# Routing, row scatters and weight splits placed inside the first attention, with split weights kept in DRAM

## The chip, the cores and the metric

One NeuronCore of one Trainium2 chip runs the whole kernel as one program. The metric is the device time of that core in microseconds (us); the time before is the median of three runs.

## The reference, cut to what matters

Two layers work on x of 8 batches x 256 x 512. The first layer, which the change is in, is a masked attention over 512 positions of width 256, and then a mixture of eight experts, of which every token takes two:

```python
x = x + _L0_ffn_ref(_L0_cond_ref(x, cond_2048, Wq, Wo), w_router, w_gate, w_up, w_down)

# the experts: 2048 tokens of width 512, E=8, F=352, K=2
probs = jax.nn.softmax(x @ w_router, axis=-1)
topk_w, topk_i = jax.lax.top_k(probs, K)
topk_w = topk_w / jnp.sum(topk_w, axis=-1, keepdims=True)
coef = jnp.einsum('tk,tke->te', topk_w, jax.nn.one_hot(topk_i, e, dtype=topk_w.dtype))
for ex in range(e):
    hid = jax.nn.silu(x @ w_gate[ex]) * (x @ w_up[ex])
    out = out + coef[:, ex:ex + 1] * (hid @ w_down[ex])
```

The second layer (another attention, then experts with low-rank additions) follows and is not changed.

## The kernel before, in words

The program is a row of blocks. In a block each of the five engines (TensorE, ScalarE, VectorE, GpSimd, SyncE) runs its own list of instructions in order, and they meet through semaphores; a block ends when all engines are through. Float32 values are multiplied as pairs of float16: a high half and the low rest, in three passes.

**`layer0_attention`** (from line 372) goes over 8 batches as a software pipeline. A batch has 32 slots. In a slot TensorE makes one bank of transposed scores (`pe_st`, line 226), ScalarE its exponential (`act_slot`, line 279), and every second slot TensorE multiplies with the values (`pe_pv`, line 239). Between the slots of batch b stand, by a list (`Core.plan`, line 91, used at line 403), steps of its neighbours. The natural scores of batch b+1 (`nat`: TensorE line 206, and VectorE takes each bank's row maxima, line 297) start at slot 10, 32 of them over the 22 slots left. The rest of batch b-1 has its slots too: reciprocal at 5, spread at 9, output projection at 11, row-major output (`rows`) at 13, router logits at 16. The query projections of b+2 are at 22 and 27. Natural and transposed scores have two banks each, and each engine keeps the order of the list, so an engine that stops holds up the others after two banks. The list is cut in two parts (at slot 18) because the loop body starts in the middle of a batch; steps of b-1 must stand ahead of the cut. SyncE's list for a batch is: load the inputs of b+2, put together its operand A (twelve DMAs, `assemble`, line 173), fetch the context of b (line 189). GpSimd puts together operand B. This kernel's attention writes row-major output for all 16 tiles of tokens to the tile `R` and the logits to `logits`.

**`layer0_routed`** (from line 729) is the next block. VectorE picks two experts for each token from all logits at once (`route_vector`, line 673, tiles of 128x128), TensorE ranks the tokens of each expert with triangular and full matrices of ones (lines 848 to 853), VectorE turns ranks into row numbers of the DRAM table `slots` and makes the table of tiles (lines 988 to 1013). GpSimd scatters the rows: 32 indirect DMAs (line 823), then 8 indirect pad writes (line 827), one behind each expert's rows. Beside this SyncE loads the weights of one expert after the other in float32 to a stage of one buffer per matrix (lines 775 to 783), ScalarE writes the high half (line 930), VectorE the low half (line 1018), and only then is the next expert's load issued. TensorE starts its first tile when all 24 low halves are made:

```python
pe.wait_ge(tabled, 1)
pe.wait_ge(consts_set, 15)
pe.wait_ge(w_lo, 3 * E)
turn_x(0)
```

SyncE issues the row loads (line 791) after its last weight load and when all scatters and pads have landed. Then come 39 tiles of 128 rows, each with two transposes, gate and up, down, and a scatter that adds to `x_rows` (line 838, GpSimd).

## Time and profile before

| what | value |
|---|---|
| median of 3 runs | 2172.78 us (2172.07 to 2174.30) |
| the profiled execution | 2166.6 us, span of its instructions 2164.5 us |
| TensorE busy | 1711.7 us (79%) |
| VectorE, ScalarE, GpSimd busy | 50%, 29%, 13% |
| DMA | 122.00 MB in 113344 packets |
| first attention | from about 11 to 525 us |
| joint: routing, splits, scatters | 525 to 623 us |
| routed tiles | 623 to 896 us |
| second layer | 896 us to the end |

The profile shows one execution. For each group of instructions it has busy time, the time of one, and what ended the idle time before. A timeline lists instructions in order of time, with merged runs of the same kind (x4 is four of them); "DMA to landing" is from a DMA's issue to its completion. PE is TensorE, ACT ScalarE, DVE VectorE, POOL GpSimd, SP SyncE; a trailing q is the engine's queue, L12 is line 12. The granted clock is in shares of TensorE's full 2.4 GHz.

### The profile page before, as it was taken

How to read it: one execution, taken by the hardware profiler on the slowest of the kernel's cores; microseconds unless marked ns; L12 is line 12 of the kernel's file. 1: busy time of each engine (PE TensorE's matmuls, PEld its weight loads, DVE VectorE, ACT ScalarE, POOL GpSimd, SP SyncE). 2: the span in 40 equal slices, each digit the busy share in tenths (PEclk: the TensorE clock that was granted, in tenths of full speed). 3: DMA queues.
4: the chain of work that ended last, by engine and by line, in shares of the span. 5: the costliest groups of instructions: out<-in, count | busy, mean ns of one | idle time of the engine just before them, and what ended most of it. 6: DMA issues, size and time to landing. Idle time of an engine off the chain costs nothing. (4 is left out here: it accounts for less than half of the span.)

```text
span 2164.5 us, 32950 instructions
## 1 busy us (share of the span) xinstructions
PE 1711.7 (79%) x10731; PEld 1023.2 (47%) x10731; DVE 1085.5 (50%) x2017; ACT 620.2 (29%) x1160; POOL 272.8 (13%) x343
## 2 busy tenths in 40 slices
PE   5888888885049999456777787795599999999998
PEld 1233333332026665232344443454477777777776
DVE  5455555542533333124455555553466665665665
ACT  0333333342332222131433333341321111111111
POOL 3111111100822222201111111000000000000000
PEclk7899999997569999756798998996699999999999
DMA  4122221101954444521111111014500000000000
GB/s 146 45 55 55 54 54 54 40 11 61 328 179 84 81 84 80 139 92 30 30 40 40 39 39 38 17 34 92 135 2 10 10 0 10 10 10 0 10 10 10
DMA packets 113344, 122.00 MB, mean 56 GB/s; under 512 B 40388, under 2 KB 79192, under 8 KB 113208
## 3 DMA queue, kind: packets, MB, share of 16 engines
q1 hardware_dynamic: 96872, 86.63, 14.1%
q0 software_dynamic: 15632, 34.30, 7.5%
q8 instruction: 43, 0.70, 0.1%
q14 instruction: 29, 0.24, 0.0%
q10 hardware_dynamic: 768, 0.13, 0.0%
HBM read 61.17 MB, written 29.96 MB: 42 GB/s over the span
## 5 line engine op out<-in xcount | busy, mean ns | idle before, releaser
L1768 ACT ACTIVATE d_SG<-d_bank 128x256 f32<-128x256 f32 x264 | 101.2, 383 | 381.0 <-PE d_bank L1705 301.9
L301 DVE TENSOR_REDUCE a_NM<-a_bn 128x1 f32<-128x512 f32 x256 | 163.4, 685 | 79.1 <-PE a_bn L215 75.6
L1803 DVE SCALAR_TENSOR_TENSOR d_HF<-d_bank,d_SG 128x256 f32<-128x256 f32 x264 | 112.1, 425 | 170.7 <-ACT d_SG L1768 152.3
L283 ACT ACTIVATE a_EX<-a_bt 128x512 f32<-128x512 f32 x256 | 143.9, 597 | 148.3 <-PE a_bt L234 147.9
L252 PE MATMUL a_bc<-a_EX,a_V 128*64 128x512 f32 x512 | 138.9, 621 | 0.0
L215 PE MATMUL a_bn<-a_B,a_A 97*128 97x512 f16 x256 | 98.3, 416 | 45.9 <-DVE a_NM L301 28.7
L1810 DVE TENSOR_TENSOR d_H_l<-d_HF,d_H_h 128x256 f16<-128x256 f32 x264 | 112.4, 426 | 9.3 <-DVE d_H_h L1808 0.4
L234 PE MATMUL a_bt<-a_A,a_B 98*128 98x512 f16 x256 | 90.7, 384 | 24.0 <-ACT a_EX L283 21.5
L301 DVE TENSOR_REDUCE c_NM<-c_bn 128x2 f32<-128x512 f32 x128 | 81.0, 681 | 42.2 <-PE c_bn L215 38.5
L862 PE MATMUL b_TX<-identh,R 128*128 128x128 f16 x312 | 24.3, 221 | 92.5 <-DVE b_wdl L1018 89.7
L1705 PE MATMUL d_bank<-XTl,d_wuh 128*128 x352 | 95.9, 273 | 0.0
L1705 PE MATMUL d_bank<-XTh,d_wuh 128*128 x352 | 95.9, 273 | 0.0
L1705 PE MATMUL d_bank<-XTh,d_wul 128*128 x352 | 95.9, 273 | 0.0
L1705 PE MATMUL d_bank<-XTh,d_wgh 128*128 x352 | 95.9, 273 | 0.0
L1705 PE MATMUL d_bank<-XTh,d_wgl 128*128 x352 | 95.9, 273 | 0.0
L1705 PE MATMUL d_bank<-XTl,d_wgh 128*128 x352 | 95.9, 273 | 0.0
L215 PEld LDWEIGHTS a_bn<-a_B,a_A 97*128 97x128 f16 x256 | 22.6, 98 | 154.4 <-DVE a_NM L301 114.0
L1230 PE MATMUL c_pp<-c_wqh,c_XNh 128*128 128x512 f16 x192 | 82.8, 431 | 12.5 <-DVE c_XNl L1340 7.8
L838 POOL DMA_INDIRECT x_rows<-R x39 | 60.5, 1550 | 224.7 <-DVE R L1028 220.8
L181 POOL DMA_DIRECT2D c_B<-c_H x64 | 35.2, 555 | 419.6 <-DVEq L1387 419.6
L1808 DVE CAST d_H_h<-d_HF 128x256 f16<-128x256 f32 x264 | 77.4, 293 | 16.1
L1668 POOL COPY d_EX<-d_kinds 128x1024 f32 x8 | 8.3, 1040 | 596.9 <-PE d_bank L1690 443.7
(346 smaller groups left out, 4044.7 us busy)
## 6 DMA issues: line engine op xcount, KB each, us to landing
R<-slot_rows SPq DMA_DIRECT2D x39, 264.0 KB
b_stage<-in_L_ffn_w_gate SPq DMA_DIRECT2D x8, 704.0 KB, 7.1
b_stage<-in_L_ffn_w_up SPq DMA_DIRECT2D x8, 704.0 KB, 7.0
a_xb<-in_x SPq DMA_DIRECT2D x8, 512.0 KB, 3.8
a_A<-a_H SPq DMA_DIRECT2D x64, 64.0 KB, 2.9
a_B<-a_H POOLq DMA_DIRECT2D x64, 64.0 KB, 2.6
a_CT<-a_CS SPq DMA_DIRECT2D x32, 128.0 KB
b_stage<-in_L_ffn_w_down SPq DMA_DIRECT2D x8, 512.0 KB
```

What stands on the lines that cost most here:

```text
L215: mm = nc.tensor.matmul(self.bn[s % 2][:, k * c.n:(k + 1) * c.n], A[0:c.k_nat, h, (t0 + k) * P:(t0 + k + 1) * P], B[0:c.k_nat, h, :], star ...
L234: mm = nc.tensor.matmul(self.bt[s % 2][:, k * c.n:(k + 1) * c.n], B[0:c.k_t, h, (t0 + k) * P:(t0 + k + 1) * P], A[0:c.k_t, h, :], start=Tr ...
L252: mm = nc.tensor.matmul(bank[64 * odd:64 * odd + 64, 0:c.n], self.V[n.par][:, t, h + odd, :], self.EX[(s + odd) % 4][:, k * c.n:(k + 1) * ...
L283: nc.scalar.activation(self.EX[s % 4][:, :], self.bt[s % 2][:, :], ACT.Exp).then_inc(self.exp_done, 1)
L301: self.nc.vector.tensor_reduce(self.NM[:, s * cols:(s + 1) * cols], self.bn[s % 2][:, :].rearrange("p (k n) -> p k n", k=cols), AX, ALU.ma ...
L838: Q.indirect_dma_start(out=g.xd[:, :], out_offset=bass.IndirectOffsetOnAxis(ap=XS[i % 4][:, E:E + 1].bitcast(I32), axis=0), in_=Y[i % 2][: ...
L1230: mm = nc.tensor.matmul(bank[:, :], xs[:, k, t * P:(t + 1) * P], ws[:, k, j * T0:(j + 1) * T0], start=(k == 0 and m == 0), stop=(k == KF - ...
L1705: mm = MM(b[:, w * CH:(w + 1) * CH], wt[s][:, k, f * P:(f + 1) * P], X[m][:, k, toks], start=(w == 0 and k == 0 and i == 0), stop=(k == KF ...
L1768: nc.scalar.activation(SG[k % 3][:, :], GU[(f + 3) % 4][:, 0:CH], ACT.Silu, scale=1.0 / WS).then_inc(silu, 1)
L1803: V.scalar_tensor_tensor(out=HF[:, :], in0=b[:, CH:2 * CH], scalar=1.0 / WS, in1=SG[k % 3][:, :], op0=ALU.mult, op1=ALU.mult).then_inc(mul ...
L1808: V.tensor_copy(H[0][:, :], HF[:, :]).then_inc(hi_step, 1)
L1810: V.tensor_tensor(H[1][:, :], HF[:, :], H[0][:, :], ALU.subtract).then_inc(hid, 1)
```

## The change

- Routing is done for one batch (two tiles of tokens) at a time, in the list of the attention. The steps of b-1 are now: `rows` at slot 12, `logit` at 14 (VectorE copies the logits and does 13 more steps to choose on 128x16 elements), `exp` at 18 (one exponential, two VectorE steps), `rank` at 21 (four matmuls, seven VectorE steps; a running count per expert is kept in `g.run`). The cut moves from slot 18 to 22.
- GpSimd makes the coefficients (five small operations) and scatters the four row tiles of b-1, waits until they have landed, and goes on to the operand of the next batch.
- Weights: in batch b the three matrices of expert b are split, by ScalarE and VectorE, at slots 1, 4 and 7. SyncE writes both halves to the DRAM table `expert_halves` and then loads the next expert's matrix; the first loads are issued after the assembly of batch 1.
- `layer0_routed` makes only the table of tiles. SyncE writes the eight pads as direct DMAs at a row number read from a register, when the table is there. ScalarE's queue loads the split weights with one DMA per expert from the start of the block, and TensorE waits for each expert's weights by a count that SyncE raises between its row loads.
- Tiles that shared the storage of `R` have their own storage now. The semaphores of the attention are cleared by GpSimd in the next block.

The diff, cut to its core:

```diff
-        plan = c.plan(18, {5: ("recip",), 9: ("spread",), 11: ("out",), 13: ("rows",), 16: ("logit",), 22: ("q0",), 27: ("q1",)},
+        plan = c.plan(22, {1: ("w0",), 4: ("w1",), 5: ("recip",), 7: ("w2",), 9: ("spread",), 11: ("out",), 12: ("rows",),
+                           14: ("logit",), 18: ("exp",), 21: ("rank",), 22: ("q0",), 27: ("q1",)},
                       ("shift", "values"))
...
+                def keep_weights(e, more=True):
+                    for i in range(3):
+                        sp.wait_ge(w_lo, 3 * e + i + 1)
+                        for h in range(2):
+                            sp.dma_start(g.halves[bass.ds(e, 1), :, h, W_AT[i]:W_AT[i] + W_SIZE[i]].rearrange("o p f -> (o p) f"),
+                                         part(h, i)).then_inc(w_kept[i], 16)
+                        if more:
+                            load_weights(e + 1, i)
...
                 a.assemble(sp, b1, a.A, a.a_in, (H, L, H))
+                sp.wait_ge(st_clear, 1)
+                for i in range(3):
+                    load_weights(0, i)
                 with sp.Fori(0, NB // 2 - 1) as i:
                     for q in range(2):
                         n = Batch(i, q + 2)
                         load(sp, n)
+                        keep_weights(2 * i + q)
                         a.assemble(sp, n, a.A, a.a_in, (H, L, H))
                         a.sp_context(sp, Batch(i, q))
...
+                    pool.wait_ge(rowed, n.idx + 1)
+                    pool.wait_ge(g.placed, n.idx + 1)
+                    pool.sem_inc(rows_begun, 1)
+                    for u in range(2):
+                        for k in range(2):
+                            Q.indirect_dma_start(out=g.slots[:, :],
+                                                 out_offset=bass.IndirectOffsetOnAxis(ap=r.place_i[:, 2 * n.par + k, u:u + 1], axis=0),
+                                                 in_=R[:, 2 * n.par + u, :], in_offset=None).then_inc(scattered, 16)
+                    pool.wait_ge(scattered, 64 * (n.idx + 1))
+                    pool.sem_inc(row_free, 1)
...
+                def split(n, i):
+                    act.wait_ge(st_in[i], (16, 16, 32)[i] * (n.idx + 1))
+                    act.wait_ge(w_kept[i], 32 * (n.idx + 1))
+                    nc.scalar.activation(part(0, i), stage[i][:, :], ACT.Copy, scale=WS).then_inc(w_hi, 1)
...
+                sp.wait_ge(tabled, 1)
                 for e in range(E):
...
+                    row = sp.value_load(r.pad_i[0:1, e:e + 1], min_val=0, max_val=E * REGION)
+                    sp.dma_start(g.slots[bass.ds(row, P), :], g.ZB[:, :]).then_inc(pads, 16)
+                sp.wait_ge(g.scattered, 64 * NB)
+                sp.wait_ge(g.pads, 32)
+                sp.wait_ge(pads, 16 * E)
+                ready = 0
                 for i in range(MT):
                     if i >= 4:
                         sp.wait_ge(added, 16 * (i - 3))
                     row = sp.value_load(r.tab[0:1, 0, i:i + 1], min_val=0, max_val=E * REGION)
                     sp.dma_start(XS[i % 4][:, :], g.slots[bass.ds(row, P), :]).then_inc(x_in[i % 4], 16)
+                    upto = (1, 1, 2, 3, 4, 6, 8)[min(i, 6)]
+                    for e in range(ready, upto):
+                        sp.wait_ge(w_in[e], 16)
+                        sp.sem_inc(w_ready, 1)
+                    ready = upto
...
                     e = pe.value_load(r.tab[0:1, 1, i:i + 1], min_val=0, max_val=E - 1)
+                    pe.wait_ge(w_ready, e + 1)
...
-                pe.wait_ge(w_lo, 3 * E)
                 turn_x(0)
...
+                for e in range(E):
+                    act.dma_start(W[:, e, :], g.halves[e].rearrange("p h f -> p (h f)")).then_inc(w_in[e], 16)
```

## Rows read from the trace of the kernel before

**Rows 1.** Table of stretches: from:to, length, busy (count) by engine, clock, DMA share, GB/s

```profile
175.00:230.00 55.00, 47.24 (x193) 16.23 (x193) 31.88 (x47) 22.39 (x40) 4.73 (x10) 1.00 0.14 37
...
533.00:623.00 90.00, 0.30 (x9) 0.24 (x6) 47.36 (x53) 32.33 (x24) 56.79 (x44) 0.50 0.87 311
...
560.00:580.00 20.00, 0.00 (x0) 0.00 (x0) 10.02 (x6) 7.66 (x7) 16.65 (x12) 0.50 1.02 374
...
623.00:896.00 273.00, 254.99 (x1833) 158.28 (x1831) 88.40 (x156) 74.70 (x118) 60.45 (x39) 0.99 0.41 73
```

**Rows 2.** Timeline of TensorE: start, us, line, tiles, [idle before <- releaser]

```profile
622.87 1.01 PE L862 MATMUL b_TX<-identh,R 128*128 128x128 f16 x8 [89.70 <-DVE b_wdl L1018]
```

**Rows 3.** Timeline of SyncE's DMA issues in the joint

```profile
525.85 0.43 SPq L775 DMA_DIRECT2D b_stage<-in_L_ffn_w_gate  x1
...
527.41 0.92 SPq L783 DMA_DIRECT2D b_stage<-in_L_ffn_w_down  x1
...
616.65 3.67 SPq L791 DMA_DIRECT2D R<-slot_rows  x4
```

**Rows 4.** Timeline of ScalarE in the joint

```profile
530.28 1.38 ACT L930 ACTIVATE b_wgh<-b_stage 128x1408 f16<-128x1408 f32 x1 [6.00 <-DMA b_stage<-in_L_ffn_w_gate]
...
535.89 1.48 ACT L930 ACTIVATE b_wdh<-b_stage 128x1536 f16<-128x1536 f32 x1 [1.80 <-DMA b_stage<-in_L_ffn_w_down]
```

**Rows 5.** Timeline of VectorE in the joint

```profile
538.01 0.18 DVE L979 TENSOR_TENSOR r_w<-r_w 128x16 f32<-128x16 f32 x1
...
538.22 0.29 DVE L980 TENSOR_TENSOR r_t<-r_oh,r_w 128x128 f32<-128x128 f32 x1
...
541.61 0.15 DVE L997 TENSOR_SCALAR r_cnt<-b_U 1x8 f32<-1x8 f32 x1
...
545.98 0.17 DVE L1013 TENSOR_SCALAR r_tab<-r_which 1x39 int32<-1x39 f32 x1
...
553.64 1.62 DVE L1018 SCALAR_TENSOR_TENSOR b_wgl<-b_stage,b_wgh 128x1408 f16<-128x1408 f32 x1 [2.75 <-ACT b_wgh L930]
```

**Rows 6.** GpSimd in the joint; then landings of line 817 and of line 838

```profile
528.04 0.63 POOL L817 DMA_DIRECT2D slot_rows<-b_ZB  x1 [0.30 <-POOL R L815]
...
543.16 1.10 POOL L823 DMA_INDIRECT slot_rows<-R,r_place_i  x1 [0.30 <-issue]
...
DMA to landing us min/median/max: 6.6/6.6/6.6
...
DMA to landing us min/median/max: 4.5/4.8/5.2
```

**Rows 7.** One attention batch: ScalarE's first exponentials, TensorE at slot 9, next batch

```profile
174.96 2.17 ACT L283 ACTIVATE a_EX<-a_bt 128x512 f32<-128x512 f32 x4 [6.13 <-PE a_bt L234]
...
182.61 1.08 PE L252 MATMUL a_bc<-a_EX,a_V 128*64 128x512 f32 x4
...
183.62 1.98 PE L264 MATMUL a_pp<-a_RV,a_SEL 8*128 8x512 f32 x4
...
233.13 2.16 ACT L283 ACTIVATE a_EX<-a_bt 128x512 f32<-128x512 f32 x4 [4.78 <-PE a_bt L234]
```

**Rows 8.** The same batch on VectorE: reciprocal and idle times before maxima and projection

```profile
179.39 3.34 DVE L322 RECIPROCAL a_RV<-a_RR 8x512 f32<-8x512 f32 x1 [5.45 <-DMA a_RR<-a_CS]
...
205.38 1.89 DVE L301 TENSOR_REDUCE a_NM<-a_bn 128x1 f32<-128x512 f32 x3 [1.18 <-PE a_bn L215]
...
208.11 1.29 DVE L301 TENSOR_REDUCE a_NM<-a_bn 128x1 f32<-128x512 f32 x2 [0.84 <-PE a_bn L215]
...
213.40 0.69 DVE L602 SCALAR_TENSOR_TENSOR a_QM<-a_pp,a_cb 128x512 f32<-128x512 f32 x1 [1.42 <-PE a_pp L488]
```

**Rows 9.** Batch 0: SyncE's last assembly DMA, and VectorE's first maximum after it

```profile
70.30 0.60 SPq L181 DMA_DIRECT2D a_A<-a_H  x1
...
75.99 1.29 DVE L301 TENSOR_REDUCE a_NM<-a_bn 128x1 f32<-128x512 f32 x2 [13.85 <-PE a_bn L215]
```

More of the change, by code:

```diff
@@ L106, in walk @@
 def walk(plan, table, b=None, b1=None, b2=None, last=None):
-    batch = {"first": b, "slot": b, "nat": b1, "shift": b1, "recip": last, "spread": last, "out": last, "rows": last, "logit": last}
+    batch = {"first": b, "slot": b, "nat": b1, "shift": b1, "recip": last, "spread": last, "out": last, "rows": last, "logit": last, "exp": last, "rank": last,
+             "w0": b, "w1": b, "w2": b}
     for name, *args in plan:
@@ L354, in batches @@
     walk(rest, steps, end, None, None)
-    walk([("recip",), ("spread",), ("out",), ("rows",), ("logit",)], steps, last=end)
+    walk([("recip",), ("spread",), ("out",), ("rows",), ("logit",), ("exp",), ("rank",)], steps, last=end)
 class Chain:
```

397 lines of the change are left out of this document (225 added, 172 removed).

## The prediction

> **What bounds the kernel now.** I read the stages first, then the engines across the joint between the first attention and the routed experts, then one batch of the attention. The table of stretches [rows 1] shows four things. In a batch of the attention TensorE is busy 47.2 of 55 us at full clock, so it is close to the bound. From 533 to 623 us it does nothing, while the DMA engines are at 0.87 of their time. At 560 to 580 they are full at 374 GB/s. From 623 to 896 TensorE is the bound again. So the joint is 90 us in which weights are loaded, split and rows scattered. Its end is set by the last low half of the weights: the first transpose of a row tile starts at 622.87, released by that split [rows 2]. All before it on the joint is the SP queue's loads [rows 3], two splits for each (ScalarE's and VectorE's [rows 4, 5]), and beside them 40 scatters on GpSimd [rows 6]. The change takes this work out of the joint. What it puts into the attention lands on engines that feed a TensorE with 7.8 us of slack in 55.
>
> **What the joint becomes.** Times are on the old axis, as if the attention had not grown. The last logits are out at about 525.2 (the routed block's first load issues at 525.85 [rows 3]). Then: 14 choosing steps (the logit copy among them) on 128x16 elements. A step and its wait take 0.21 us (538.01 to 538.22 [rows 5]), so 2.9, to 528.1; four small matmuls, 0.5, an estimate; seven ranking steps, 1.5, to 530.1; GpSimd starts at about 530.4. The exponential and GpSimd's coefficients run beside the ranking. Four scatters at 1.10 busy plus 0.30 [rows 6], 5.6, so the last is issued at 534.6; it lands 4.8 later if it is like the row additions [rows 6], 539.4, and GpSimd waits for that before the block ends. With 0.4 for the change of block the eight weight loads start at 539.8. The table of tiles is 17 steps: 15 run from 541.61 to 546.15 [rows 5], two more are 0.4, so it is there at 544.8. Then SP writes eight pads, each with a register load: the four row loads after 616.65 start 1.11 apart ((3.67 - 0.33)/3 [rows 3]; one issue is 0.33), so 8.9 us, to 553.7.
>
> **When the pads land** decides the sign. The first row load waits for them. Weights are 8 x 128 rows of 17,408 bytes, 17.8 MB, queued at once on ScalarE's queue from 539.8; the pads are 2.2 MB in rows of 2,112 bytes on SP's queue. The two ends: if both queues share by bytes, a pad lands in what the one plain pad write took beside loads, 6.6 us [rows 6], the last at 552.6 + 6.6 = 559.2, and with 3.5 for the first row load (0.7 at full rate, 2.5 fixed, see below, 0.3 to issue) the first transpose starts at 562.7, 60 us earlier than now. If a small write has to let a large transfer pass each time, the eight pads are through only with the eight weight loads: 20.0 MB at 374 GB/s [rows 1] is 53.5 us, 541 + 53.5 = 594.5, plus 3.5 gives 598, 25 us earlier than now. I take the second. The row that is nearest: the plain pad write of 264 KB was issued at 528.04, when 2.2 MB of loads had been issued from 525.85 to 528.3, and landed at 534.6 [rows 3, 6]. The last of those loads released ScalarE at 535.9 [rows 4]. All of it (2.75 MB with the second write) needs 7.4 us at 374 GB/s, to about 534.5. The first load, 704 KB alone, landed 4.4 after its issue [rows 3, 4], of which 1.9 is transfer at that rate, so 2.5 is fixed. An equal share by bytes would have had the pad write there in 1.4 + 2.5 = 3.9; it came out with the last of the loads. Here the rows in front are eight to twelve times longer still.
>
> The Trainium skill bears on this choice ("DMA: Bandwidth & Descriptors", Queues, rings and completion order): a DMA engine takes turns between its queues by whole packets, not by bytes, so long rows win against short ones; by that the first transpose is the one at 598. The same page's advice to prefer transfers of 1 MiB and more (Bandwidth) speaks for the change's one load per expert, and by it alone the one at 562.7 would hold. No row of this trace has rows of 17 KB beside short ones, so neither is shown here.
>
> **What the attention pays**, a batch at a time.
> (a) Weight halves on ScalarE at slots 1, 4 and 7: two of 1.38 and one of 1.48 [rows 4], 4.24 us. In slots 0 to 9 ScalarE's exponentials (ten of 0.54) fill 5.4 of the 7.65 us from 174.96 to the fifth pair of value matmuls at 182.61 [rows 7]. With the halves it is 9.65: these slots become ScalarE's, and TensorE is 2.1 us later. Bounds: 0.2 if the matmuls ran that much ahead (they can't: two banks of scores), 4.24 if all is exposed.
> (b) VectorE's low halves, 1.62 each [rows 5], lie in slots without maxima. But reciprocal and spread are there. The reciprocal began at 179.39 [rows 8] when its rows came. Now it stands behind the second low half, from 182.3 to 185.6; TensorE reaches the spread at 183.62 [rows 7] + 2.1 = 185.7, so it is covered, just. The third low half is behind it and makes the spread's product 0.4 late. That is the price of (b); without that cover it is up to 2.9.
> (c) The 14 choosing steps, 2.9 us where there was the one logit copy, now stand between two maxima. VectorE sat idle 1.18 before the maximum that follows the copy [rows 8]; the rest, 1.6, and 0.2 for waits and increments, goes to TensorE, which has two banks of natural scores and runs dry.
> (d) The two steps after the exponential, 0.45, fit the 0.84 that VectorE idles after an even slot [rows 8]: 0. The exponential itself is ready by then.
> (e) The seven ranking steps, 1.5, come where VectorE waits 1.42 for the query projection [rows 8]: 0.1, and 0.3 with TensorE's four matmuls.
> (f) GpSimd holds the four scatters from slot 21 to about 12 us later (5.6 plus 4.8 and the wait); the next batch's rows are assembled at slot 29, about 14 us after slot 21, so nobody waits: 0. If the scatters take 1.6 or more each the rows are late, but they have 8 us until slot 10.
> (g) SP: six writes, four loads and their waits end by slot 8; its next job is at slot 29: 0. The 4.4 MB a batch fit, since the DMA engines are at 0.14 [rows 1].
> Sum for each of batches 1 to 6: 2.1 + 0.4 + 1.8 + 0.1 + 0.3 = 4.7, 28.2 in all. Batch 7 has no maxima beside it: 2.6.
> (h) Batch 0 starts with nothing loaded: the loads of expert 0 stand on SP behind the assembly of batch 1, whose last DMA issues at 70.30 [rows 9]. So they issue at 71.0 to 73.3, and land as the first ones did, the first after 4.4, the last 8.5 after its issue [rows 3, 4]: 75.4 and 81.1. ScalarE has meanwhile stopped at slot 1. From 81.1 there are 1.48, two exponentials and the value matmuls, to about 85.0. Today the first maximum of the next batch is at 75.99, after its own wait of 13.85 [rows 9], from matmuls at 75.35. So 9.4, and 2 for the low clock after that pause, an estimate. With 0.4 for the added constant load at the start: 11.8.
> Attention: 28.2 + 2.6 + 11.8 = 42.6 us. Bounds: 20 (only batch 0 and 1 us a batch), 70 (splits, choosing and ranking all exposed, 9.1 on seven batches, less the cover of the waits).
>
> **The sum.** 42.6 lost, 24.9 won (622.9 - 598): 17.7 slower. The profiled execution has a span of 2164.5 and took 2166.6; the median of the runs is 2172.78, 6.2 above that, and I keep this distance. 2172.8 + 17.7 = 2190.5, rounded to 2190; the new profile's own time would be about 2184. The routed stage itself (273 us, [rows 1]) is unchanged: same matmuls, one more wait a tile, and weights that are all in by then.
>
> **Rivals.**
> Rival 1, on the other side: pads and row loads get through by share of bytes. Then the first transpose is 60 us earlier, at 562.7, and the place is the same pad wait on SP. Against it the pad row above; for it, that the trace never shows rows as long as these, so the slow end is carried over from one write. The weight loads would then run beside the first five or six tiles, whose additions already land only 4.8 after issue at 6.6 us a tile; I charge 4 us. 2172.8 + 42.6 - 56 = 2159.4, range 2148 to 2172. It decides from the point where the last pad lands before about 577, which is where the gain equals 42.6.
> Rival 2: the added steps hide better than I count, 20 us in the attention, with slow pads: 2172.8 + 20 - 25 = 2168. For it: each engine but TensorE is under 60% busy [rows 1]. Against: the waits are in sequence, with two banks.
> Rival 3: the scatters make the rows of the next batch late, or GpSimd and VectorE slow each other: 3 us more in six batches, 2190 + 18 = 2208. For it the uneven durations of scatters beside VectorE's long steps; against it the 8 us of slack in (f).
>
> **How the numbers follow.** Forecast 0.54 (2177 to 2204), rival 1 0.29, rival 2 0.09, rival 3 0.08. A measurement of this kernel tells about 0.2% (4.3 us) from no change. Faster: 0.26 of rival 1 and half of rival 2, 0.30. Same: 0.03 + 0.03 + 0.02 of the forecast, 0.08. Slower: 0.62. The range leaves out the lowest part of rival 1 and the upper half of rival 3: 2151 to 2207. The likeliest case's own range is 2177 to 2204.
>
> **What would show it.** In the changed profile: the last of SP's eight pads lands only when the weights' last load does (more than 40 us after the weights' start), and the first transpose follows it by 3 to 4 us; if it lands within 15 us of its issue, rival 1 holds. Batches 1 to 6 should last 63 us instead of 58.2 from one first exponential to the next (174.96 to 233.13 [rows 7]); in slots 0 to 9 the fifth pair of value matmuls comes 9.7 us after the first exponential; before the maximum that follows the choosing TensorE is idle near 2 us. Batch 0's slot 1 ends in a wait of some 14 us for the first gate weights. I am wrong in sign if the pads come early, and in size if a batch costs under 3 or over 7 us.

## The result, and the profile after

The changed kernel takes 2212.95 us (median of 4 runs, 2204.91 to 2214.55), the kernel before 2173.54 (2172.07 to 2174.89). The ratio is 1.0173, 95% interval 1.0153 to 1.0193: 39.4 us slower, where 17.7 was forecast. The sign was right; the time lies above the range (2151 to 2207). The two profiled executions have spans of 2212.6 and 2164.5, so 48.1 us are to be found in them; the profiled one is the slowest of its four, and the kernel's own runs differ by up to 10 us. Every ratio in the experiments is to runs of the kernel before that were made beside them (medians 2170.8 to 2173.3); "less" and "more" in us are against the changed kernel's 2212.95 and carry those few us of difference too.

First the joint, which answers to [rows 2 to 4]. Timeline rows of TensorE, SyncE and ScalarE; then the drains of GpSimd's queue at the end of the attention block (line of the block, duration in ns min/median/max, start in us), first before, then after; then issues and landings (KB each, median us):

```profile
668.04 1.01 PE L1018 MATMUL b_TX<-identh,b_XS 128*128 128x128 f16 x8 [72.61 <-DMA b_XS<-slot_rows]
620.48 8.22 SPq L977 DMA_DIRECT2D slot_rows<-ZB  x8
665.22 3.83 SPq L986 DMA_DIRECT2D b_XS<-slot_rows  x4
614.67 4.16 ACTq L1082 DMA_DIRECT2D b_W<-expert_halves  x8
...
L410 POOLq DRAIN  x1: 9716/9716/9716, 409.4 to 409.4; - x1
...
L431 POOLq DRAIN  x1: 9540/9540/9540, 604.9 to 604.9; - x1
...
b_W<-expert_halves ACTq DMA_DIRECT2D x8, 2176.0 KB, 26.7
slot_rows<-ZB SPq DMA_DIRECT2D x8, 264.0 KB, 26.6
...
slot_rows<-ZB SPq DMA_DIRECT2D x2, 264.0 KB, 36.2
```

What the DMA engines moved for the two queues from 625 to 660 us in the changed kernel (q10 has the weights, q1 the pads; packets, MB, share of the 16 engines):

```profile
q10 hardware_dynamic: 865, 13.39, 89.3%
q1 hardware_dynamic: 862, 1.62, 11.9%
```

The eight pads are issued from 620.5 to 628.7; the first lands after 10.2 us, the last two after 36.2, at 664.5, with the weights' last load. The two queues got the same number of packets (865 and 862), and the weights' packets carried eight times as many bytes (15.5 KB on the mean against 1.9): the pads did not wait for the queue of weights as a whole, they shared it packet by packet. The row loads go out at 665.2 and the first transpose is at 668.0. And GpSimd's queue drains for 9.54 us, from 604.9 to 614.5, while nothing else runs: every engine starts the routed block behind it. Before the change the same drain was at 409.4, under the attention.

Then the attention. Both fences below are tables of stretches as in [rows 1]. The first is six batches, from one shift-row store (ScalarE's DMA at line 187 before, 191 after, one a batch) to the sixth after it: before, and after.

```profile
111.74:458.17 346.43, 299.01 (x1224) 108.44 (x1223) 196.09 (x288) 134.42 (x240) 48.23 (x90) 1.00 0.18 47
...
120.44:521.03 400.59, 329.35 (x1248) 114.92 (x1247) 246.09 (x438) 157.70 (x264) 82.73 (x145) 0.93 0.39 123
```

Six batches last 54.2 us longer: TensorE idles 71.2 instead of 47.4 us (+23.8) and is busy 329.4 instead of 299.0 (+30.4), with only 24 more small matmuls. The last column but two tells why the busy time grew: the granted clock was 1.00, now it is 0.93 on the mean. Single batches after, the first of these six and the second, and one of the half-clock pieces in the second:

```profile
120.44:183.15 62.71, 51.33 (x210) 18.55 (x209) 41.59 (x74) 26.25 (x44) 14.30 (x26) 1.00 0.42 135
183.15:257.82 74.67, 60.73 (x211) 20.32 (x211) 41.72 (x74) 26.26 (x44) 14.10 (x26) 0.86 0.35 113
...
200.30:207.10 6.80, 6.80 (x15) 2.38 (x14) 3.15 (x5) 0.00 (x0) 0.00 (x0) 0.50 1.04 405
```

At full clock a batch lasts 62.7 (63 was forecast, 58.4 is its length before). In the second the clock falls to 1.2 GHz four times, for 3 to 7 us each, and one more thing is there: VectorE stands 3.4 us with nothing to wait for, and TensorE behind it (two rows each):

```profile
238.42 0.69 DVE L305 TENSOR_REDUCE a_NM<-a_bn 128x1 f32<-128x512 f32 x1 [3.42 <-issue]
374.08 0.69 DVE L305 TENSOR_REDUCE a_NM<-a_bn 128x1 f32<-128x512 f32 x1 [3.14 <-issue]
...
239.17 0.39 PE L219 MATMUL a_bn<-a_B,a_A 97*128 97x512 f16 x1 [2.43 <-DVE a_NM L305]
241.67 0.61 PE L219 MATMUL a_bn<-a_B,a_A 97*128 97x512 f16 x1 [1.89 <-DVE a_NM L305]
```

Both stalls begin, at 235.0 and 370.9, where the loop jumps back (the cut before slot 22), right behind the ranking steps. There is one at both jumps back of VectorE's loop and none where the loop is left.

The whole span: attention (to the last context load, 500.24 before, 567.05 after) +66.8; from there to the first transpose 101.0 where the forecast had 97.8 us, and 122.6 before, -21.6; routed stage, to the landing of the last row addition, +4.9; rest -1.9. Of the 4.9, the first tile at the lower clock takes 0.5 (8.5 us instead of 8.0 from one tile's first transpose to the next); most tiles last 6.69 us where they lasted 6.60, and some single ones over 7.5. The prediction had this stage unchanged, with one more wait a tile at no cost; no run tells whether that wait is the cause. Of the last -1.9, 1.8 is the drain of GpSimd's queue at the end of the routed block, which stands in the open in both kernels, before and then after:

```profile
L767 POOLq DRAIN  x1: 8401/8401/8401, 893.8 to 893.8; - x1
...
L971 POOLq DRAIN  x1: 6623/6623/6623, 943.8 to 943.8; - x1
```

### The profile page after: what moved, and what is told of

It is laid out like the page before. It is cut to its first block and busy times, and to the rows that moved or that the text cites. A ratio compares the mean times of both kernels' runs of the same rounds, so it can differ in the third digit from the quotient of the medians.

```text
span 2212.6 us, 33741 instructions
## 1 busy us (share of the span) xinstructions
PE 1743.5 (79%) x10731; PEld 1029.9 (47%) x10731; DVE 1104.0 (50%) x2167; ACT 617.8 (28%) x1167; POOL 260.9 (12%) x375
## 5 line engine op out<-in xcount | busy, mean ns | idle before, releaser
L219 PE MATMUL a_bn<-a_B,a_A 97*128 97x512 f16 x256 | 105.1, 438 | 58.6 <-DVE a_NM L305 47.4
L256 PE MATMUL a_bc<-a_EX,a_V 128*64 128x512 f32 x512 | 149.5, 665 | 0.0
L238 PE MATMUL a_bt<-a_A,a_B 98*128 98x512 f16 x256 | 100.0, 408 | 46.8 <-ACT a_EX L287 42.7
L1150 DVE SCALAR_TENSOR_TENSOR b_HF<-b_U,b_SG 128x352 f32<-128x352 f32 x39 | 20.4, 524 | 149.3 <-issue 88.0
L1004 POOL DMA_INDIRECT x_rows<-b_Y,b_XS x39 | 60.7, 1557 | 269.4 <-DVE b_Y L1141 260.0
L1033 PE MATMUL b_G<-b_W,b_XT 128*128 x468 | 78.2, 318 | 10.5 <-issue 10.5
```

What stands on the lines that cost most here:

```text
L219: mm = nc.tensor.matmul(self.bn[s % 2][:, k * c.n:(k + 1) * c.n], A[0:c.k_nat, h, (t0 + k) * P:(t0 + k + 1) * P], B[0:c.k_nat, h, :], star ...
L238: mm = nc.tensor.matmul(self.bt[s % 2][:, k * c.n:(k + 1) * c.n], B[0:c.k_t, h, (t0 + k) * P:(t0 + k + 1) * P], A[0:c.k_t, h, :], start=Tr ...
L256: mm = nc.tensor.matmul(bank[64 * odd:64 * odd + 64, 0:c.n], self.V[n.par][:, t, h + odd, :], self.EX[(s + odd) % 4][:, k * c.n:(k + 1) * ...
```

## Experiments on the joint

The theory at this point: the pads wait because the two queues take turns by rows, and GpSimd's drain stands in the open. The rivals: the pad stores are slow by themselves, or wait for the whole queue of weights.

**Pads and four rows ahead of seven weight loads.**

```diff
                 for e in range(E):
+                    if e == 1:
+                        for k in range(4):
+                            act.wait_ge(x_in[k], 16)
                     act.dma_start(W[:, e, :], ...).then_inc(w_in[e], 16)
...
-                    upto = (1, 1, 2, 3, 4, 6, 8)[min(i, 6)]
+                    upto = (0, 0, 0, 3, 4, 6, 8)[min(i, 6)]
```

> Edit: ScalarE issues expert 0's weights at once, the other seven only when the first four row loads have landed; all else as in the changed kernel (2212.95 us; pads issued at 620.5 to 628.7, the last landed at 664.5, first transpose at 668.0). Theory (turns): the pads are late because they share the DMA engines with 17.8 MB of long rows. Then each pad lands some 3 us after its issue, the first transpose is at about 635, and the seven loads run from 638 to 675 (15.6 MB at 430 GB/s). The fifth tile's row load falls under them and lands near 676 where the fifth tile began at 695 before: about 18 us less, 2195. Rival (the stores are slow by themselves, or SP's register loads hold them): the last pad still lands over 20 us after its issue, the first transpose stays near 660 to 668 and the weights come later on top: 2213 to 2230.

Measured: 2190.66 us, ratio 1.0079 (1.006 to 1.0098), 22 less than the changed kernel.

```profile
slot_rows<-ZB SPq DMA_DIRECT2D x8, 264.0 KB, 2.2
...
633.05 1.01 PE L1018 MATMUL b_TX<-identh,b_XS 128*128 128x128 f16 x8 [38.79 <-DMA b_XS<-slot_rows]
679.64 1.03 PE L1018 MATMUL b_TX<-identh,b_XS 128*128 128x128 f16 x8 [11.77 <-DMA b_XS<-slot_rows]
```

A pad now lands in 2.2 us. The stores are not slow by themselves: it was the weight loads. The price came where expected, a wait of 11.8 in the fifth tile.

**Short rows.** Weights in DRAM as 12 pieces of 1408 or 1536 bytes a partition, with gaps, loaded by four transfers an expert.

```diff
-        g.halves = dram("expert_halves", (E, P, 2, W_ALL), F16)
+        g.halves = dram("expert_halves", (E, P, 12, 800), F16)
...
+                    for h in range(2):
+                        at = h * W_ALL
+                        act.dma_start(W[:, e, at:at + 2 * GU].rearrange("p (c f) -> p c f", c=4),
+                                      g.halves[e, :, 6 * h:6 * h + 4, 0:GU // 2]).then_inc(w_in[e], 16)
+                        act.dma_start(W[:, e, at + 2 * GU:at + W_ALL].rearrange("p (c f) -> p c f", c=2),
+                                      g.halves[e, :, 6 * h + 4:6 * h + 6, 0:DN // 2]).then_inc(w_in[e], 16)
```

> Edit: the split weights lie in DRAM in rows of 1408 and 1536 bytes with gaps (17,408 bytes in one piece before) and are loaded by four transfers an expert; nothing else. Theory (a DMA engine takes turns between the two queues by rows, so the length of a row decides): the pads' rows of 2112 bytes now are the longer ones, each pad lands 3 to 5 us after its issue, first transpose at 636 instead of 668, the tiles then run beside the weight loads: 25 to 30 us less, 2185. Rival 1 (turns by whole transfers, or by bytes of a fixed chunk): the last pad lands some 10 to 20 us after issue, first transpose 645 to 655. Rival 2 (the later queue simply waits until the earlier one is empty): no change, last pad with the last weights, 668 to 672.

Measured: 2203.35 us, ratio 1.0156 (1.0117 to 1.0194), only 10 less.

```profile
slot_rows<-ZB SPq DMA_DIRECT2D x8, 264.0 KB, 5.8
...
635.03 1.01 PE L1018 MATMUL b_TX<-identh,b_XS 128*128 128x128 f16 x8 [46.41 <-DMA b_XS<-slot_rows]
...
656.27 1.64 ACTq L1086 DMA_DIRECT2D b_W<-expert_halves  x1
657.96 1.02 ACT L1094 ACTIVATE b_XT<-b_TX 128x1024 f16<-128x1024 f16 x1 [69.42 <-issue]
```

The theory of turns holds: with shorter rows beside them the pads land in 5.8 instead of 26.6 us (3 to 5 were expected), and the 865 packets beside 862 in the changed kernel say the same. The Trainium skill's rule of turns by whole packets ("DMA: Bandwidth & Descriptors", Queues, rings and completion order) agrees. That the first transpose came at 635.0 where 636 was expected is partly luck. In this run the block began 6.8 us earlier (first weight load issued at 607.9 instead of 614.7), so from there to the first transpose it took 27.2 us, where the expectation had 21.3 and the changed kernel 53.4. But the time didn't follow: 32 issues take ScalarE until 657.9 (before, eight took 4.2 us): the first nine take 0.4 to 1.7 us each, the tenth 5.8, and from there on they go out about as fast as the transfers themselves (12 MB in 37 us). The copy of the first tile stands behind them on the same engine. The gain went into a new wait; this I had not seen.

**GpSimd's last scatters behind the block's end.** The last batch's coefficients and four scatters move to the start of the routed block.

```diff
                 route(Batch(NB // 2 - 1, 0))
-                route(Batch(NB // 2 - 1, 1))
...
+                head = R[:, 2:4, :]
+                did(Q.tensor_copy(head[:, :, E:E + 1]..., last.token[:, :]))
+                did(Q.tensor_tensor(last.c[:, :, :], last.oh2[:, :, :], each(last.ex[:, :]), ALU.mult))
+                did(Q.tensor_tensor(last.c[:, :, :], last.c[:, :, :], last.oh1[:, :, :], ALU.add))
+                did(Q.tensor_tensor(head[:, :, 0:E], last.c[:, :, :], each(last.inv[:, :]), ALU.mult))
+                for u in range(2):
+                    for k in range(2):
+                        Q.indirect_dma_start(out=g.slots[:, :], ..., in_=R[:, 2 + u, :], in_offset=None).then_inc(g.scattered, 16)
```

> Edit: GpSimd's work for the last batch (coefficients, four scatters) stands at the start of the routed block instead of at the end of the attention block. In the changed kernel GpSimd's drain at the block's end takes 9.54 us (604.9 to 614.5) and everything waits for it. Theory (hidden drain): GpSimd ends the attention block under the last batch, its drain is covered, the routed block starts some 0.4 after the last placement (597.2) instead of at 614.7, the weight loads end 17 us earlier, the scatters hide behind the pads: 2213 - 17 = 2196. Rival (the drain is a cost of the block's end itself, begun only when all engines are there): the block starts at 607, 8 us less (the landing of the scatters alone), 2205.

Measured: 2192.41 us, ratio 1.0092 (1.0075 to 1.0109), 20.5 less. The drain (block line, ns, start):

```profile
L430 POOLq DRAIN  x1: 9213/9213/9213, 565.7 to 565.7; - x1
L430 ACTq DRAIN  x1: 232/232/232, 591.8 to 591.8; - x1
```

It still takes 9.2 us, but from 565.7, under the last batch; the block starts at 594.2 instead of 614.5. It belongs to GpSimd's end of a block, not to the block's common end. Other blocks of the same profiles show that not every end costs this: 8.4 and 6.6 us at the end of the routed block (before, after), 9.1 at the end of the second attention, under 0.2 us in blocks in which GpSimd issued one or two DMAs, 1.0 at the program's end. What sets its length no run here shows.

**Both, with weights paced.** Expert 0's load at once, expert 1's when four rows have landed, one more in each of six tiles.

> Edit: the late last route of the run before (2192 us), and the weights paced: expert 0's load at the block's start, expert 1's when the first four row loads have landed, one more in each of the next six tiles. Theory (turns, and both edits add up): the block starts at 597, the pads are issued from 602 to 611 and land within 3 to 4 us, the first transpose is at 617 to 620 where the changed kernel had 668, and no later row load has more than one or two weight loads (2.2 MB, 5 us each) in front of it, under the slack of four row buffers: 2213 - 49 = 2164, below the kernel before. Rival (GpSimd's late scatters now end the joint, or each row load stands behind a weight load and stops TensorE in tiles 1 to 8): 2175 to 2185.

Measured: 2176.46 us, ratio 1.0029 (1.0011 to 1.0047). First transpose at 619.2, as expected, 49 us earlier than in the changed kernel, but the total is 36 less: from first transpose to last row addition it takes 293.3 us (276.0 in the changed kernel).

```profile
658.53 1.03 PE L1033 MATMUL b_TX<-identh,b_XS 128*128 128x128 f16 x8 [7.01 <-DMA b_XS<-slot_rows]
679.88 1.03 PE L1033 MATMUL b_TX<-identh,b_XS 128*128 128x128 f16 x8 [5.62 <-DMA b_XS<-slot_rows]
```

## Experiments on the attention

**Splits left out** (the routed experts then compute with zeros).

> Edit: the 48 split instructions of the attention are left out (weights are zeros), their loads and stores in DRAM and the waits for these are kept; so the routed experts' output is wrong and only the time is read. Theory A (as in the prediction: ScalarE's halves cost 2.1 a batch, the low halves 0.4, each at full clock): 7 x 2.5 = 17.5 less, 2195, and the granted clock between 200 and 540 us stays where it was (pieces at 0.5 in most batches). Theory B (the pauses that the splits cut into TensorE's work are what lowers the clock): the clock is 1.00 in batches 1 to 6, the batches last 60 to 61 us, 35 to 45 less, 2170. Theory C (the pause after the choosing steps lowers the clock): clock and batches like A's, and the half-clock pieces begin right behind that pause.

Measured: 2197.95 us, ratio 1.0119 (1.0091 to 1.0147), near theory A's 2195, though not by its terms, as the rows below show.

**Choosing and ranking left out** (no row is routed, every tile reads expert 0).

> Edit: VectorE's choosing steps (13 a batch) and ranking steps (7) in the attention are left out, all else stays: logit copy, matmuls, scatters (to fixed places), splits. So no row is routed and every tile reads expert 0: the output is wrong and only the attention is read. Theory (this is the share of a batch that the splits don't have: leaving out the splits took only 0.6 to 0.8 us off a batch at full clock, 62.7 to 62.1, where before the change it was 58.4): batches at full clock last 59 to 60 us, TensorE's pause of 2.1 behind the choosing is gone, the stalls of VectorE at the jump back are shorter, the clock is 1.00 in most batches, and the attention ends at about 525 instead of 567. Rival (the prediction's terms: splits 2.5, choosing and ranking 2.2): batches of 60.8 us at full clock, half-clock pieces as before, the end at 545 to 550.

**Neither splits nor weight traffic** (zeros once; routing as in the changed kernel).

> Edit: no splits, and no loads and stores of weights in the attention either (expert 0's zeros are stored once and loaded for all experts, so the output is wrong); routing as in the changed kernel. Theory D (traffic lowers the clock): 1.00 in batches 1 to 7, each 62 long, the attention ends near 530. Theory P (TensorE's pauses): the same share of half clock as with the splits alone left out (mean 0.95 over batches 2 to 7), the end earlier than that run's 548.6 only by batch 0, whose wait for the first weights (9 us) is gone: 538 to 541.

Measured, the six batches of these three in this order (the whole times of the last two, 2175.52 and 2198.60 us, ratios 1.0017 and 1.0127, say little, their experts don't do the kernel's work):

```profile
120.34:505.48 385.14, 314.56 (x1248) 111.22 (x1247) 217.34 (x420) 136.10 (x246) 80.54 (x145) 0.96 0.40 128
...
121.15:487.43 366.28, 311.02 (x1248) 111.32 (x1247) 224.78 (x318) 156.88 (x264) 80.17 (x145) 0.98 0.43 134
...
116.13:509.67 393.54, 321.99 (x1248) 112.55 (x1247) 217.88 (x420) 136.18 (x246) 79.56 (x145) 0.94 0.21 58
```

Without splits: 385.1 where the changed kernel has 400.6, the clock up from 0.93 to 0.96; batches at full clock last 62.15 (62.7 with splits). So the splits cost 0.6 a batch, not 2.5; the rest of their 15 us is clock. Without choosing and ranking: 366.3, batches at full clock of 60.65 and 61.0, so choosing and ranking cost 1.9 (2.2 was the sum of the prediction's (c), (d) and (e)), VectorE's stall is gone in both places, and the last three batches are at 1.00. It is the larger share by far: 34 of the 54 us. The end of the attention, 530.9, lies between what the two theories said (525 and 545). Without the traffic the clock is no higher: 0.94, and the stall is there (3.5 and 3.3). So nothing here speaks for the traffic as a cause of the low clock (one profile of each kernel); the end, 553.8, was 13 later than the other theory had it, since the stalls and half-clock pieces weighed more than in the run without splits (0.96).

Where TensorE waits in one batch at full clock (total us, times, longest), changed kernel, then without choosing, then without splits:

```profile
PE a_bn L219 <- DVE a_NM L305: 6.3, 8, 2.1
PE a_bt L238 <- ACT a_EX L287: 3.9, 5, 1.2
...
PE a_bn L219 <- DVE a_NM L305: 4.0, 8, 1.1
PE a_bt L238 <- ACT a_EX L287: 3.9, 5, 1.2
...
PE a_bn L219 <- DVE a_NM L305: 6.8, 8, 2.1
PE a_bt L238 <- ACT a_EX L287: 2.9, 3, 1.2
PE a_pp L268 <- DVE a_RV L326: 0.5, 1, 0.5
```

The choosing steps are the 2.3 more behind the maxima, ScalarE's halves 1.0 behind the exponentials, not 2.1. The prediction had a test for the halves, the fifth pair of value matmuls 9.7 us after the first exponential. Changed kernel, then without splits, both in the batch at full clock:

```profile
124.00 1.09 ACT L287 ACTIVATE a_EX<-a_bt 128x512 f32<-128x512 f32 x2 [4.84 <-PE a_bt L238]
133.47 1.08 PE L256 MATMUL a_bc<-a_EX,a_V 128*64 128x512 f32 x4
...
124.14 2.16 ACT L287 ACTIVATE a_EX<-a_bt 128x512 f32<-128x512 f32 x4 [5.08 <-PE a_bt L238]
131.78 1.08 PE L256 MATMUL a_bc<-a_EX,a_V 128*64 128x512 f32 x4
```

It is 9.5 us with the halves and 7.6 without. So up to slot 9 the prediction's mechanism and its size are right, 1.8 us; but only 0.6 of them are left at the end of the batch. Without splits TensorE waits 0.5 for the reciprocal and 0.5 more behind the maxima: the forecast added up delays of which the later ones partly cover the earlier.

**The cut at slot 18 again, and VectorE's loop written out** (the body of the loop is the same, named `two`).

```diff
-        plan = c.plan(22, {..., 18: ("exp",), 21: ("rank",), ...
+        plan = c.plan(18, {..., 16: ("exp",), 17: ("rank",), ...
```

> Edit: the loop over batches is cut before slot 18 as in the kernel before, not before slot 22; the exponential's step stands at slot 16 and the ranking at 17. In the changed kernel VectorE stands 3.4 us in batch 2 and 3.1 us in batch 4 with nothing to wait for, right at the cut. Theory A (the edge of the loop costs VectorE these 3 us and a slow clock behind it; at slot 18 it has a pause anyway, as before): 3 to 5 us less in batches 2, 4 and 6, in all 10 to 15, 2200. Rival (the edge costs the same wherever it is, or the stall is due to the longer program): same time within 5 us, the stall stands at slot 18.

```diff
+    if flat:
+        for i in range(NB // 2 - 1):
+            two(i)
+    else:
+        with eng.Fori(0, NB // 2 - 1) as i:
+            two(i)
...
+            batches(eng, c, plan, pre, values_of, table, opening, flat=eng is nc.vector)
```

> Edit: VectorE's loop over batches in the first attention is written out (its instructions in a row, no jump back), the other engines' loops stay. Theory (the 3.2 to 3.4 us in which VectorE stands without a wait are the jump back to the start of a long loop body): both stalls, in batches 2 and 4, are gone, and with them TensorE's pauses of 2.4 and 1.9 and some of the half clock behind them: 7 us at least, 2195 to 2206. Rival (the stall belongs to the stretch of short ranking steps, which VectorE goes through faster than they can be fetched): stalls of 1 to 3 us stand at the same place in all of batches 1 to 6, and the time is the same or worse, 2213 to 2225.

Measured: cut at 18, 2216.91 us, ratio 1.0204 (1.017 to 1.0238); written out, 2198.4, ratio 1.013 (1.0097 to 1.0162). With the cut moved the stall moved too:

```profile
235.23 2.68 DVE L305 TENSOR_REDUCE a_NM<-a_bn 128x1 f32<-128x512 f32 x4 [3.20 <-issue]
...
118.98:502.48 383.50, 316.07 (x1248) 111.65 (x1247) 246.31 (x438) 157.74 (x264) 81.84 (x145) 0.97 0.41 128
```

The second row is the six batches of the loop written out: 383.5 instead of 400.6, the clock 0.97, no stall left. So the stall needs the jump back; since it is absent at the same jump when the 20 small steps are left out, and in the kernel before, it also needs them (a longer body, or short steps right ahead of the jump; these two were not told apart). From one jump back to the next VectorE's trace has about 360 records in every kernel with the stall, 278 without choosing and 257 in the kernel before, both without it. The moved cut's time, 2216.91, is its rival's (same within 5 us), the written-out loop's is the theory's.

**Choosing in three pieces** (slots 14, 16 and 17).

> Edit: the 14 choosing steps of VectorE in slot 14 are split in three, first choice in slot 14, second in 16, sums in 17. Theory C (TensorE's pause of 2.1 us behind the choosing steps sets off part of the half-clock pieces): the pause falls to under 1.2 in each batch, batches 1 to 6 are 1 us shorter at full clock and the granted clock rises from 0.93 on the mean of 183 to 521 us: 10 to 18 us less, 2195 to 2203. Rival (VectorE's load as a whole, and the jump back, do it): under 6 us less, 2207 to 2213, mean clock unchanged.

Measured: 2204.17 us, ratio 1.0156 (1.0121 to 1.0192), six batches in 392.2, mean clock 0.95: 9 less, just short of what the theory asked, and little more than such stretches vary (see below). The pause of 2.1 behind the choosing is gone in every batch, the clock is not back: that pause alone is not what lowers it.

**TensorE's pauses filled** with seven matmuls that nobody reads.

```diff
+                def fill(uses, times):
+                    pe.wait_ge(a.proj_out, uses.base + uses.k + 1)
+                    bank = a.pp[(uses.parity + uses.k) % 2]
+                    for _ in range(times):
+                        nc.tensor.matmul(bank[:, :], wT[:, 0, 0, 0:P], wT[:, 1, :, :], start=True, stop=True)
```

> Edit: seven matmuls a batch whose result nobody reads (128x512, f32, some 0.43 us each at full clock) stand on TensorE right before its longest pauses: three in slot 15, two each in slots 23 and 28, 3.0 us a batch. Theory P (the pauses lower the clock): batches 2 to 7 stay at 1.00, last 63 to 64 us, and the attention ends near 550 to 555 instead of 567, though TensorE does more: 2197 to 2202. Theory D (the weight traffic, or TensorE's work as a whole, lowers it): the half-clock pieces stay and the extra matmuls cost up to 3 us a batch where they are longer than the pause: 2213 to 2230.

Measured: 2212.63 us, ratio 1.0191 (1.0176 to 1.0205): no change. The six batches, and the added matmuls in them (busy us, mean ns):

```profile
121.85:521.57 399.72, 349.92 (x1332) 129.85 (x1331) 246.53 (x438) 157.03 (x264) 80.45 (x144) 0.97 0.39 123
...
L667 PE MATMUL a_pp<-a_wT 128*128 128x512 f32 x84 | 40.5, 611 | 0.0
```

The clock rose from 0.93 to 0.97 though nothing but work in the pauses was added. But that work was over twice what was planned: a float32 matmul stands in the trace as two rows, so the 42 are 84, and they kept TensorE busy 6.8 us a batch, not 3.0. In six batches they cost 40.5 us; TensorE's waits fell by 21 (from 69 to 48) and its other matmuls, at the higher clock, by 20. So the pauses are a cause of the low clock, but not all of it: VectorE's two stalls stayed (TensorE still waits 2.52 at the first), and half-clock pieces with them. In the kernel of the next section with the loop written out and the choosing in pieces (2156.79 us) neither the stalls nor that pause is left, and the six batches are still at 0.97 on the mean, one of them at 0.88 and 69.9 us long; what lowers the clock there stays open. How the pieces fall is partly chance: five kernels with the same attention as the changed one and stores of the same or nearly the same shape have six batches of 394 to 401 us.

**High halves on GpSimd instead of ScalarE.**

```diff
+                def halves(n):
+                    for i in range(3):
+                        pool.wait_ge(st_in[i], (16, 16, 32)[i] * (n.idx + 1))
+                        pool.wait_ge(w_kept[i], 32 * (n.idx + 1))
+                        pool.sem_inc(rows_begun, 1)
+                        Q.tensor_scalar(part(0, i), stage[i][:, :], WS, None, ALU.mult).then_inc(w_hi, 1)
```

> Edit: the high halves of the weights are made by GpSimd (between its rows and its scatters) instead of ScalarE; VectorE's low halves stay. Theory (ScalarE's halves hold up its exponentials in slots 0 to 9, and GpSimd idles some 36 us a batch): as leaving the splits out, 15 us less, 2198, with a GpSimd half near 1.4 us (its copy of 128x1024 elements took 1.04). Rival (GpSimd and VectorE hold each other up): halves of 3 us or more, VectorE's maxima longer beside them, scatters and rows later, 2213 to 2240.

Measured: 2272.94 us, ratio 1.0449 (1.0424 to 1.0473), 60 slower. Groups of instructions from 100 to 500 us (count, busy us, mean ns); the last row is VectorE's low half in the changed kernel:

```profile
L549 POOL TENSOR_SCALAR a_WHL<-a_stage 128x1408 f16<-128x1408 f32 x10 | 37.6, 3768 | 0.4
L564 POOL TENSOR_SCALAR r_token<-r_token 128x2 f32<-128x2 f32 x5 | 23.6, 4711 | 1.0 <-POOL a_R L563 1.0
L855 DVE SCALAR_TENSOR_TENSOR a_WHL<-a_stage,a_WHL 128x1408 f16<-128x1408 f32 x10 | 45.4, 4575 | 27.4 <-POOL a_WHL L549 27.4
L855 DVE SCALAR_TENSOR_TENSOR a_WHL<-a_stage,a_WHL 128x1536 f16<-128x1536 f32 x5 | 8.4, 1681 | 0.0
...
L852 DVE SCALAR_TENSOR_TENSOR a_WHL<-a_stage,a_WHL 128x1408 f16<-128x1408 f32 x12 | 19.5, 1625 | 22.1 <-ACT a_WHL L702 22.1
```

The rival holds. VectorE's two low halves that run beside GpSimd's next half take 4.58 instead of 1.63 us, the third, beside a step on 128x2 numbers only, 1.68. That step, which runs beside VectorE's reciprocal and third low half, takes 4.7 (0.46 in the changed kernel). And GpSimd's half by itself takes 3.77 us where 1.4 was expected, which is a loss without any contention. The Trainium skill ("GPSIMD Engine Reference", Specifications) names contention between GpSimd and VectorE's instructions with two inputs in SBUF; the low half is one, and the trace agrees.

## Putting it together

**Late route, earlier pads (as soon as their places are known), paced weights, pieces, loop written out**, without and with the halves on GpSimd:

> Edit: the changed kernel with late route, VectorE's loop written out, choosing in three pieces, paced weight loads (expert 1 only after the first row tile is taken, then one in each of six tiles, SP waiting for each expert one tile later), and the pads issued as soon as their places are known (not with the whole table). Theory (the gains of the single edits add up): joint 36.5, written-out loop 14.5, pieces 9 are 60 less, and 4 for the earlier pads, 4 for the row loads that stood behind SP's waits: 2213 - 68 = 2145, first transpose at 595 to 600. Rival (loop and pieces both win back the same lost clock, and the row loads stay behind weight loads): 2155 to 2165.

> Edit: as best1, and the high halves on GpSimd as in pool_halves. Theory (ScalarE's share is separate from VectorE's): 10 to 15 less than best1, 2133. Rival (GpSimd and VectorE in each other's way): more than best1, 2155 to 2170.

Measured: 2156.79 us, ratio 0.9914 (0.9891 to 0.9936), and 2226.16, ratio 1.0239 (1.022 to 1.0258). The first is faster than the kernel before by 0.9%, though 12 us short of the sum, where its rival stood: the pieces add nothing beside the loop written out (six batches in 382.2, 383.5 without them; 377 to 382 in the four kernels that have both), and the routed stage takes 291.4.

**A weight load in every second tile; then eight row buffers instead of four, with loads paced by tile or in one burst.**

> Edit: as best1 (2157 us, fastest so far), but a weight load in every second tile, not in every one. Theory (in best1 TensorE waits 6.3 and 6.8 us for a row load in tiles 4 and 6, because a weight load is in front of the row additions, 7.2 instead of 4.9 us, and of the row loads, 6.2 instead of 2.7): both waits fall to 2 or less, 10 us less, 2147. Rival (one weight load in front of a row addition is enough to break the four-buffer chain, whenever it comes): 2 to 4 such waits of 3 us remain over twelve tiles, 2153 to 2160.

> Edit: as best1 (2157 us), with eight row buffers instead of four; the first eight row loads are issued before expert 1's weights, the other weights one in each of the six tiles after. Theory (in best1 each row load waits for the addition four tiles back, and both stand behind a weight load: TensorE waits 6.3 and 6.8 us): those two waits are gone, the stage from first transpose to last addition is 276 to 280 instead of 291: 2157 - 13 = 2144. Rival (the additions, 7.2 us each beside a weight load where a tile lasts 6.7, pace the tiles through the two output buffers): TensorE waits for VectorE's output or the addition instead, 288 to 292, 2155.

> Edit: as best4, but the weights of experts 1 to 7 in one burst once the first eight rows are in (15.2 MB, some 36 us). Theory (a burst delays row loads and additions of five tiles, eight rows are already there, and behind it nothing is delayed): like best4 within 4 us, 2140 to 2148. Rival (the additions of the first five tiles stand behind up to seven weight loads each and hold the output buffers): one wait of 15 to 25 us in tile 2 or 3, 2160 to 2170.

Measured: every second tile 2179.64 (1.0038, 1.0025 to 1.0051), its stage 314.2 us with five waits of 4.7 to 7.0 for a row load. There the five loads that stand alone cost one such wait each, and the two close together at the start none; one in every tile, the seven cost two. Eight buffers, paced: 2154.75 (0.9915, 0.9895 to 0.9934), stage 282.8; in one burst: 2157.51 (0.9931, 0.9911 to 0.995), stage 285.8. The waits for rows are gone, and part of what the rivals said comes in their place (VectorE's output of a tile waits for the addition two tiles back):

```profile
652.85 0.75 DVE L1181 TENSOR_SCALAR b_Y<-b_O,b_XS 128x512 f32<-128x512 f32 x1 [9.14 <-DMA x_rows<-b_Y,b_XS]
```

So of the 13 us that were expected of the buffers, the stage gave 9, and the run 2, which is within its noise.

## Why the prediction was right in sign and wrong in size

- **When the pads land**: right. "I take the second" gave 53.5 us from the weights' start to the last pad; it was 49.8, since the loads run at 417 to 434 GB/s, not at the 374 of [rows 1]. Rival 1 was wrong, and the last pad's landing (36.2), the first transpose 3.5 us behind it, the equal numbers of packets and the run with short rows show it. (The sum let the loads start at 541, its own working at 539.8.)
- **"0.4 for the change of block"**: the failed step of the joint, +9.1. [rows 6] told how GpSimd scatters, but I never looked at what its queue does at a block's end. The drain of 9.7 us was in the trace of before, at 409.4, where it was hidden. The 0.4 had no row for GpSimd's queue behind it. Faster weights (-3.7) and scatters that landed in 2.8 instead of 4.8 (-2) took back some: in all +3.2. The run with the late route shows the step: drain covered, 20.5 us less.
- **(a), (b)**: 2.5 forecast, 0.6 measured at full clock. Up to slot 9 the delay is 1.8 of the 2.1 (9.65 less 7.65 is 2.0), but the sum carried it whole to the batch's end, and most of it is covered there.
- **(c), (d), (e)**: 2.2 forecast, 1.9 measured, the pause behind the choosing 2.12 (near 2 forecast). A full-clock batch is 4.3 longer, 4.7 was forecast; of this 0.6 and 1.9 are told by the runs, at most 0.7 are the four ranking matmuls, about 1 stays open. So that 4.3 and 4.7 lie so close is in part luck: one term was four times too large, and something of 1 us was in no term.
- **(f), (g)**: held as far as the batches go: nobody waited for scatters or for SyncE.
- **(h)**: batch 0 lost 8.7 to the next shift-row store, 11.8 was forecast (its 9.4 should be 9.65 by its own numbers); ScalarE's wait was 14.6 (some 14 forecast).
- **The clock and the jump back**: the failed step of the attention, terms that the sum put at nothing. Every term but (h) was worked out at the clock of [rows 7, 8], 1.00, and none had VectorE standing at its loop's jump back. I had charged low clock once, after the pause of batch 0. In the changed kernel eleven half-clock pieces lie between 183 and 504 us, TensorE's busy time is 30 us longer, of which some 3 are new matmuls, and VectorE stands twice for over 3 us. Six batches at 4.3 more each would be 26 us longer; they are 54.2 longer, and 28.2 was forecast. With 3.1 less in batch 0 and 1.3 more behind the six, that is the 24 us between 42.6 and 66.8. Without the stalls and with the pauses cut (loop written out, pieces) six batches take 18 to 23.5 us less for the same work. How much each of the two costs by itself is not settled beyond the 14.5 us of the loop written out.
- **Rival 3** named 18 us more for engines slowing each other. The attention took 24 more, so the size was near, by luck; the mechanism wasn't: neither late rows nor contention, but VectorE's jump back and TensorE's clock.
- **The profiled execution**: 30.4 of its excess are 24.2 (attention), 3.2 (joint), 4.9 (routed tiles, see above) less 1.9. The medians are 39.4 apart where the profiles are 48.1: before's profile was 6.2 under its median, and this one the slowest of its four runs.

## What to carry to other kernels

Before costing a move to a block's end, look up every queue's drain at the block ends of the old trace, hidden ones too. A step put between two matmuls of an engine near its bound costs its microseconds and can cost the clock too, as it did here: cost it once at full clock and once with a stretch at half clock behind it. Small stores that gate the work go ahead of bulk loads, and bulk loads go out on a queue whose engine has nothing else to do until they are through.

## What was not expected of the hardware

- GpSimd's queue drained for 9.2 to 9.7 us at its end of the first attention, whenever that came (9.72 before, 9.54 after, 9.21 with the late route), and for 6.6 to 9.1 at the ends of two other blocks in which it had issued many DMAs.
- VectorE stood 3.1 to 3.5 us without a wait at each jump back of its loop once 20 short steps a batch were in it; written out, the same instructions had no such stall.
- GpSimd and VectorE held each other up: VectorE's low half went from 1.63 to 4.58 us, GpSimd's step on 128x2 numbers from 0.46 to 4.7.
- With more transfers queued, ScalarE's own DMA issues held it up: 8 took 4.2 us, 32 of the same bytes some 50.
- A row addition and a row load issued right behind a weight load of 2.2 MB took 8.9 to 9.4 and 9.1 to 9.2 us instead of 4.9 and 2.7 (loop written out, paced weights), enough for one wait of 5 to 7 us with four buffers. The 7.2 and 6.2 of the expectations are medians of one such and one undisturbed.
- Two DMA queues with work got the same number of packets, 865 and 862 in 35 us, and so 13.4 and 1.6 MB.
